# Attention on one core: value products in blocks of four steps, eight probability tiles

## The chip, the core and the metric

The kernel runs as one launch on one core of a Trainium2 chip. The metric is the device time of that launch in microseconds, the median of the runs. The engines are TensorE (PE, with its weight loads shown apart as PEld), VectorE (DVE), ScalarE (ACT), GpSimd (POOL) and SyncE (SP, which issues the DMAs); each works through its own queue in order and they meet at semaphores.

## The reference

Two batches of 2048 tokens with 256 features pass through an attention block and then a two-layer local-attention and MLP block, each inside an adaptive layer norm. The change touches only the first attention:

```python
x: (2, 2048, 256); 16 heads of 64
h = layernorm(x) * (1 + ca) + sa
q, k, v = heads(h @ Wq + bq), heads(h @ Wk + bk), heads(h @ Wv + bv)
pattern = einsum('bhid,bhjd->bhij', k, q) / 8
prob = softmax(pattern, axis=-2)          # over the keys i
out = einsum('bhis,bhid->bhsd', prob, v)
x = x + ga * (concat(out) @ Wo + bo)
# then: layernorm, and a gated block of two layers of windowed attention and gated MLP
```

## The kernel before

**Phases.** A start-up (input, first projections, the first head's maxima), then attention, then the second layer norm and the two layers. Only attention is written by the code that changes. It takes 32 heads one after the other (2 batches by 16 heads); two heads are a pair, `hh` 0 and 1, and there are 16 pairs. `PLAN` has four kinds of pair: FIRST, MIDDLE (13 of them, in hardware loops), BRIDGE (the last of batch 0, which also turns the next batch's hidden tokens into `hT`), LAST.

**A head.** The 2048 queries are taken in two halves (`cp` 0 and 1) of 1024, the 2048 keys in 16 tiles of 128 (`kt`), so a head has 32 steps (`STEPS`). For a step:

- `scores`: four matmuls of 512 columns on the whole 128x128 array (L1430 and L1431, reduced-precision fp32, the high part and the low part of the operands), into one of two pairs of PSUM banks. Step t waits for the exponentials of step t-2, which free its banks.
- ScalarE takes one exponential of 128x1024 (L848) and writes `prob[t % PRING]`. It waits for the tile to be free again: the value products of step t-PRING and the addition of that tile.
- `values`: PE multiplies the tile with `vv` (L1442), full fp32, 64 output columns, one query half on each half of the array side by side. The page counts two records for each such matmul, so a step has four records; the two halves run at the same time.
- the column sums of the softmax: VectorE adds the tiles of `SUM_DVE` (4 of 16) to `acc_d` (L1099; the first is a copy, L1101), GpSimd the others to `acc_p` (L708) and joins both (L704).

Beside this, PE prepares the next head: `max`, 64 products of one matmul each (L1402), which exist only to find the largest score of each key row; VectorE reduces each from PSUM (L1076, 128x512). At a head's end all 64 are reduced once more, turned (`turn`, L1408), negated (`max_neg`, L1086) and sent by a DMA of SP (`qlm<-nmx`) into row 64 of `qlm`; the next head's first scores wait for it. `proj_qk` projects queries and keys for the head after next (four items of four records, L1379; ScalarE and VectorE read them, L799 to L802 and L1037 to L1039), `proj_v` the values for the next pair (L1387), `out` the output projection of the pair before (8 items, L1461 and L1120), `sum` turns an accumulator into column sums (L1451, ones times `accp`), and VectorE then takes the reciprocal (L1105, 128x512) and scales `o_raw` into `oT` (L1110): `normalise`.

**The ring.** `max`, `sum`, `turn`, `turn_h`, `proj_v` and `out` share three PSUM banks (`RING = 3`) in the order of the plan. PE may write an item only when VectorE has finished the item three places before it (`ring_slot`). For `sum` that is the end of the second L1110.

**The order.** `head_order` writes one list for a head, and PE and VectorE both follow it. Before the change it has 16 groups of two steps: two score steps, with maxima ahead, between and behind (`mm S m S mm` in most groups, where S is a score step and m a maximum), and then two value steps (`VV`). VectorE's addition stands where the values stand. `sum` of half 0 stands behind group 10, and group 11 has no maxima (but in BRIDGE, where it has `mm S m S m` and a turned tile), group 12 two or three, group 15 none: there the order is turn, the four `proj_qk`, `VV`, and for `hh` 1 `proj_v`, then `sum` of half 1.

## Time and profile before

| | us |
|---|---|
| median of 3 runs | 4878.4 (4864.67 to 4885.79) |
| the profiled execution: its own time | 4883.0 |
| its span in the profile | 4881.1 |
| attention, first value product to last | 100.9 to 3148.4 |
| PE busy over the span | 4565.5 (94%) |
| DVE / ACT / POOL busy | 3426.1 / 2212.1 / 2728.9 |
| granted TensorE clock, mean | 0.971 |

The page's busy time of PE is a union of modelled spans: a 512-column matmul is drawn with 0.40 us though the next starts 0.23 us later, so a PE that looks busy can still be losing time. What it loses is read from the distance between starts in the timeline.

### The profile page before, as it was taken

To read this page: it belongs to the slowest core of one execution; us is meant where nothing else is said; L and a number is where in the kernel's file an instruction comes from. 1 tells how busy PE (TensorE), PEld (TensorE's weight loads), DVE (VectorE), ACT (ScalarE), POOL (GpSimd) and SP (SyncE) were. 2 spreads that over 40 slices of the span, in tenths; PEclk is the share of its full clock that TensorE was granted. 3 is DMA by queue.
4 is the path that set the end of the run, shared out by engine and by line. 5 is a ranking of instruction groups with operands and counts; after the bars stand their busy time and mean duration, and the time that the engine had idled before them with its cause. 6 is when DMAs were issued, how large, how long until landed. Compare 5 with 4: busy or idle time off the path is not lost.

```text
span 4881.1 us, 65202 instructions
## 1 busy us (share of the span) xinstructions
PE 4565.5 (94%) x21552; PEld 2792.1 (57%) x21552; DVE 3426.1 (70%) x4564; ACT 2212.1 (45%) x3535; POOL 2728.9 (56%) x1172
## 2 busy tenths in 40 slices
PE   7999999999999999999999999858999897999898
PEld 5555555555555555555555555426766675777576
DVE  7887878778788788787787787565555454666354
ACT  5444444444444444444444444325665343656442
POOL 3655656566556665675666565606666223666322
PEclk9999999999999999999999999979999998999898
DMA  2000000000000000000000000010000100000001
GB/s 65 1 5 5 2 6 1 6 6 1 6 5 2 5 1 6 6 1 6 5 2 6 5 2 2 1 56 1 1 1 1 36 1 18 1 1 1 1 0 35
DMA packets 56826, 37.55 MB, mean 8 GB/s; under 512 B 32572, under 2 KB 55056, under 8 KB 56464
## 3 DMA queue, kind: packets, MB, share of 16 engines
q1 hardware_dynamic: 56464, 33.02, 2.3%
q8 instruction: 191, 3.13, 0.3%
q14 instruction: 171, 1.40, 0.1%
HBM read 28.54 MB, written 4.19 MB: 7 GB/s over the span
## 4 chain that ended last, share of the span: by engine, by line
POOL 48%; issue 26%; PE 13%; DVE 7%; ACT 4%; POOLq 1%; DMA 0%; DVEq 0%; SPq 0%; ACTq 0%
POOL accp L708 36%; PE psum L1705 4%; POOL lp L730 4%; PE psum L1580 3%; POOL accp L704 3%; POOL rnorm L720 2%; POOL qk_u L725 2%; DVE ssq L1180 1%; ACT lp L894 1%; PE psum L1626 1%; ACT qk_sq L878 1%; PE psum L1718 1%; DVE qk_w L1192 1%; DVE lneg L1206 1%; PE psum L411 1%
## 5 line engine op out<-in xcount | busy, mean ns | idle before, releaser
L708 POOL TENSOR_TENSOR accp<-accp,prob 128x1024 f32<-128x1024 f32 x640 | 1618.9, 2530 | 684.3 <-ACT prob L848 651.9
L848 ACT ACTIVATE prob<-psum 128x1024 f32<-128x1024 f32 x1024 | 1042.7, 1026 | 1547.4 <-PE psum L1431 1395.8
L1076 DVE TENSOR_REDUCE mx<-psum 128x1 f32<-128x512 f32 x1984 | 1276.0, 684 | 420.3 <-PE psum L1402 354.7
L1442 PE MATMUL psum<-prob,vv 128*64 128x512 f32 x4096 | 996.0, 607 | 0.0
L1430 PE MATMUL psum<-qhh,klh 128*128 128x512 f32 x2048 | 829.4, 405 | 39.8 <-issue 20.7
L1431 PE MATMUL psum<-qlm,kh 65*128 65x512 f32 x2048 | 818.0, 399 | 0.0
L1402 PE MATMUL psum<-klh,qhh 128*128 128x512 f32 x1984 | 711.3, 419 | 14.2 <-DVE mx L1076 10.0
L1402 PEld LDWEIGHTS psum<-klh,qhh 128*128 128x128 f32 x1984 | 347.9, 190 | 413.9 <-DVE mx L1076 245.4
L1442 PEld LDWEIGHTS psum<-prob,vv 128*64 128x64 f32 x4096 | 249.5, 136 | 513.1 <-issue 370.2
L1430 PEld LDWEIGHTS psum<-qhh,klh 128*128 128x128 f32 x2048 | 392.2, 191 | 199.8 <-issue 87.2
L1431 PEld LDWEIGHTS psum<-qlm,kh 65*128 65x128 f32 x2048 | 391.7, 191 | 91.7 <-issue 7.0
L730 POOL TENSOR_TENSOR lp<-lp,lrcp 128x1024 f32<-128x1024 f32 x128 | 301.0, 2352 | 229.8 <-DVE lrcp L1212 229.8
L1099 DVE TENSOR_TENSOR accd<-accd,prob 128x1024 f32<-128x1024 f32 x192 | 398.9, 2078 | 21.5 <-ACT prob L848 20.4
L708 POOL TENSOR_TENSOR accp<-prob 128x1024 f32<-128x1024 f32 x64 | 152.9, 2389 | 378.9 <-ACT prob L848 373.8
L720 POOL TENSOR_TENSOR rnorm<-ssc,minus_half 128x16 f32<-128x16 f32 x64 | 186.0, 2906 | 291.2 <-DVE ssc L1182 291.2
L758 POOL TENSOR_TENSOR ug_l<-uf,ug_h 128x512 fp32r<-128x512 f32 x96 | 128.6, 1339 | 387.3 <-ACT ug_h L969 387.3
L894 ACT ACTIVATE lp<-psum,lneg 128x256 f32<-128x256 f32 x512 | 236.1, 481 | 98.8 <-DVE lneg L1206 98.8
L1105 DVE RECIPROCAL psum<-psum 128x512 f32<-128x512 f32 x64 | 215.1, 3360 | 27.8 <-PE psum L1451 27.1
L1379 PE MATMUL psum<-hT,wqk 128*128 128x512 f32 x512 | 226.4, 594 | 0.0
L1626 PE MATMUL psum<-identf,lp 128*128 128x128 f32 x1024 | 144.6, 286 | 57.6 <-POOL lp L730 57.6
L1180 DVE TENSOR_REDUCE ssq<-qk_sq 128x16 f32<-128x1024 f32 x64 | 78.1, 1220 | 169.7 <-ACT qk_sq L878 169.6
L704 POOL TENSOR_TENSOR accp<-accp,accd 128x1024 f32<-128x1024 f32 x64 | 151.7, 2371 | 72.4 <-DVE accd L1099 72.1
(190 smaller groups left out, 6534.1 us busy)
## 6 DMA issues: line engine op xcount, KB each, us to landing
rot_l<-const_rot SPq DMA_DIRECT2D x2, 2048.0 KB, 8.5
out<-lpT SPq DMA_DIRECT2D x32, 128.0 KB, 1.8
wqkv_l<-L_ffn_wqkv SPq DMA_DIRECT2D x4, 768.0 KB, 9.7
w_l<-L_ffn_w SPq DMA_DIRECT2D x4, 682.0 KB
wqk<-L_attn_Wq SPq DMA_DIRECT2D x32, 64.0 KB, 2.1
wqk<-L_attn_Wk SPq DMA_DIRECT2D x32, 64.0 KB, 2.0
wv_p<-L_attn_Wv SPq DMA_DIRECT2D x16, 128.0 KB, 2.2
wo_p<-L_attn_Wo SPq DMA_DIRECT2D x16, 128.0 KB, 2.0
```

The costliest lines, as they stand in the source:

```text
L704: pool.tensor_tensor(acc_p[cp][:], acc_p[cp][:], acc_d[cp][:], ALU.add).then_inc(pool_sum, 1)
L708: pool.tensor_tensor(acc_p[cp][:], first[:], prob[kt % PRING][:], ALU.add).then_inc(pool_sum, 1)
L720: pool.tensor_tensor(rnorm[:], ssc[:], minus_half[:, 0:1].broadcast_to([P, 2 * LHEADS]), ALU.pow).then_inc(rn_done, 1)
L730: pool.tensor_tensor(lp[:, hs, :], lp[:, hs, :], lrcp[:, hs].unsqueeze(2).broadcast_to([P, IH, 2 * WIN]), ALU.mult).then_inc(lp_done, 1)
L848: act.activation(prob[t % PRING][:], psum[:, S_BANK + 2 * (t % 2):S_BANK + 2 * (t % 2) + 2, :].rearrange("p a b -> p (a b)"), ACT.Exp, sca ...
L894: op = act.activation(lp[:, hh, :], psum[:, 2 * it + h // 2, (h % 2) * 2 * WIN:(h % 2 + 1) * 2 * WIN], ACT.Exp, bias=lneg[:, hh:hh + 1], s ...
L1076: dve.tensor_reduce(mx4[:, j // CHUNKS, j % CHUNKS:j % CHUNKS + 1], ps, AX_X, ALU.max).then_inc(ring_free, 1)
L1099: dve.tensor_tensor(acc_d[cp][:], acc_d[cp][:], prob[kt % PRING][:], ALU.add).then_inc(dve_sum, 1)
L1402: pe.matmul(ps, qhh[s][:, qt * P:(qt + 1) * P], klh[s][:, c * T:(c + 1) * T], start=True, stop=True).then_inc(ring_full, 1)
L1430: pe.matmul(ps, klh[s][:, keys], qhh[s][:, cols], start=True, stop=False)
L1431: mm = pe.matmul(ps, kh1[s][:, keys], qlm[s][:, cols], start=False, stop=True)
L1442: mm = pe.matmul(psum[j * DH:(j + 1) * DH, O_BANK, :], vv[:, kt, s * DH:(s + 1) * DH], prob[t % PRING][:, j * T:(j + 1) * T], start=(kt == ...
```

## The change

- `PRING` goes from 4 to 8. The four new tiles take the place in SBUF of the start-up's `x_tail` and one `squares`, which now lie in `prob` 4 to 7; so ScalarE waits for `h1_ok` before the first exponential.
- A group has four steps (`VALUES = 4`): 8 groups a head. In a full group the order is `S mmm S mm S mmm S mm`, VectorE's addition (`a`), `VVVV`, for 10 maxima (9 and two `out` in the four groups that have them, 11 in group 5 of `hh` 0, 5 to 7 in group 0, 6 or 7 in group 6, 3 or 4 in group 7).
- `sum` of half 0 stands behind group 5, after value step 23 (before: after step 21). In group 0 and in group 6 the maxima come late: `S S m S mm S mmm` in group 6 of `hh` 1 (6 maxima), `S S m S mmm S mmm` in that of `hh` 0 (7).
- The additions of VectorE have places of their own in the order (`("add", t)`), ahead of the group's value products; in the last group ahead of `proj_qk`.
- The last group has maxima, and ends `a`, two `proj_qk`, turn, two `proj_qk`, `VVVV`; the value products of the last four steps all lie behind the projections (before: two ahead of them and two behind).
- In BRIDGE the eight turned tiles go two to a group, in groups 3 to 6; the outputs stay in groups 1 to 4, two to each.

Here `a` is an addition and `V` the value products of one step. The diff:

```diff
--- before.py
+++ after.py
@@ -35,7 +35,7 @@
 KT = N // P
 CP = CHUNKS // 2
 STEPS = CP * KT
-PRING = 4
+PRING = 8
 SUM_DVE = (2, 5, 8, 12)
 SUM_POOL = tuple(k for k in range(KT) if k not in SUM_DVE)
 
@@ -172,13 +172,12 @@
         mx1 = sb("mx1", [P, KT], at=att)
         nmx = sb("nmx", [KT, P], F32R, at=att)
         wmod_sb = hT[:, :, 0:6 * D]
-        x_tail = sb("x_tail", [P, 12, D], at=att)
         st_sum = sb("st_sum", [P, KT], at=att)
         st_neg = sb("st_neg", [P, B, KT], at=att)
         st_ssq = sb("st_ssq", [P, B, KT], at=att)
         st_var = sb("st_var", [P, B, KT], at=att)
         st_rs = sb("st_rs", [P, B, KT], at=att)
-        squares = [sb("squares", [P, 2, D], at=att), o_raw[0][:].rearrange("p (t d) -> p t d", d=D)]
+        squares = [prob[7][:, 0:2 * D].rearrange("p (t d) -> p t d", d=D), o_raw[0][:].rearrange("p (t d) -> p t d", d=D)]
         copies = o_raw[1][:].rearrange("p (t d) -> p t d", d=D)
 
 
@@ -186,7 +185,7 @@
             return t[:].rearrange("p (t d) -> p t d", d=D)
 
         x_quads = [[quad(t) for t in acc_p + acc_d],
-                   [x_tail[:, 4 * q:4 * q + 4, :] for q in range(3)] + [x_last[:]]]
+                   [quad(t) for t in prob[4:7]] + [x_last[:]]]
         h_quads = [[quad(t) for t in prob], [h_next[:, 4 * q:4 * q + 4, :] for q in range(QUADS)]]
         wo_all = oT[:].rearrange("p (k n) -> p k n", n=D)
         att.close()
@@ -294,49 +293,61 @@
 
 
 
-        GROUPS = STEPS // 2
-        SUM0_GROUP = (KT + 5) // 2
-
-        def max_places(outs):
-
-
-            weight = [4] * (GROUPS - 1) + [0]
-            weight[0] = 1
-            weight[SUM0_GROUP + 1:SUM0_GROUP + 3] = [0, 2]
-            for g in outs:
-                weight[g] = 3
+        VALUES = 4
+        GROUPS = STEPS // VALUES
+        SUM0_GROUP = (KT + 5) // VALUES
+        OUT_GROUPS, OUT_EACH = 4, 2
+        TURN_EACH = 2
+
+        def max_places(outs, turns):
+
+
+            weight = [10] * GROUPS
+            weight[0], weight[SUM0_GROUP + 1], weight[GROUPS - 1] = 5, 6, 4
+            for g in (*outs, *turns):
+                weight[g] -= 2
             return [-(-RING_MAX * sum(weight[:g + 1]) // sum(weight)) for g in range(GROUPS)]
 
+        def spread(g, n, count):
+
+            ends = [0, n // 5, 3 * n // 5, n] if g in (0, SUM0_GROUP + 1) else [-(-n * (j + 1) // count) for j in range(count)]
+            return list(zip([0] + ends, ends))
+
         FIRST, MIDDLE, BRIDGE, LAST = 0, 1, 2, 3
-        TURN_GROUP = 1 + WO_ITEMS // 2
+        TURN_GROUP = 3
 
         def head_order(which, hh):
             last = which == LAST
             maxima, projects = not (last and hh), not last
-            outs = () if which == FIRST or hh else range(1, 1 + WO_ITEMS // 2)
-            turns = range(TURN_GROUP, TURN_GROUP + TWINS) if which == BRIDGE and hh == 0 else ()
-            placed = max_places([*outs, *turns])
+            outs = () if which == FIRST or hh else range(1, 1 + OUT_GROUPS)
+            turns = range(TURN_GROUP, TURN_GROUP + TWINS // TURN_EACH) if which == BRIDGE and hh == 0 else ()
+            placed = max_places(outs, turns)
             order = [("scores", 0), ("scores", 1)]
             for g in range(GROUPS):
                 upto = placed[g] if maxima else 0
                 done = (placed[g - 1] if g else 0) if maxima else 0
                 tiles = [("max", j) for j in range(done, upto)]
                 if g in outs:
-                    tiles += [("out", 2 * (g - 1)), ("out", 2 * (g - 1) + 1)]
+                    tiles += [("out", OUT_EACH * (g - 1) + j) for j in range(OUT_EACH)]
                 if g in turns:
-                    tiles.append(("turn_h", g - TURN_GROUP))
-
-                n = len(tiles)
-                cut0 = (n + 1) // 3
-                cut1 = cut0 + n // 3
+                    tiles += [("turn_h", TURN_EACH * (g - TURN_GROUP) + j) for j in range(TURN_EACH)]
+
+                adds = [("add", t) for t in range(VALUES * g, VALUES * (g + 1)) if t % KT in SUM_DVE]
                 if g + 1 < GROUPS:
-                    order += tiles[:cut0] + [("scores", 2 * g + 2)] + tiles[cut0:cut1] + [("scores", 2 * g + 3)] + tiles[cut1:]
+                    for j, (lo, hi) in enumerate(spread(g, len(tiles), VALUES)):
+                        order += [("scores", VALUES * (g + 1) - 2 + j)] + tiles[lo:hi]
+                    order += adds
                 else:
+                    for j, (lo, hi) in enumerate(spread(g, len(tiles), 2)):
+                        order += [("scores", STEPS - 2 + j)] + tiles[lo:hi]
+                    order += adds
+                    if projects:
+                        order += [("proj_qk", i) for i in range(2)]
                     if maxima:
                         order.append(("turn", 0))
                     if projects:
-                        order += [("proj_qk", i) for i in range(QK_ITEMS)]
-                order += [("values", 2 * g), ("values", 2 * g + 1)]
+                        order += [("proj_qk", i) for i in range(2, QK_ITEMS)]
+                order += [("values", VALUES * g + j) for j in range(VALUES)]
                 if g == SUM0_GROUP:
                     order.append(("sum", 0))
             if projects and hh == 1:
@@ -835,6 +846,8 @@
                 act.wait_ge(oT_ready, G * CP + cp + 1)
                 act.activation(o_raw[cp][:], psum[:, O_BANK, :], ACT.Copy).then_inc(o_free, 1)
 
+            act.wait_ge(h1_ok, QUADS - 1)
+
             def exps(G):
                 for t in range(STEPS):
                     act.wait_ge(s_full, G * STEPS + t + 1)
@@ -1132,10 +1145,9 @@
                             max_neg(G + 1, rb, r, TURN_PLACES[hh])
                         elif kind == "turn_h":
                             next_hidden(rb, r, j, places(kind, j, hh))
-                        elif kind == "values":
+                        elif kind == "add":
                             cp, kt = divmod(j, KT)
-                            if kt in SUM_DVE:
-                                add_sum(G, cp, SUM_DVE.index(kt))
+                            add_sum(G, cp, SUM_DVE.index(kt))
                         elif kind == "sum":
                             normalise(G, rb, r, hh, j)
                         elif kind == "proj_qk":
```

## Rows read from the trace of the kernel before

**Rows 1.** The page: busy time of each engine, share of the span, instructions.

```profile
PE 4565.5 (94%) x21552; PEld 2792.1 (57%) x21552; DVE 3426.1 (70%) x4564; ACT 2212.1 (45%) x3535; POOL 2728.9 (56%) x1172
```

**Rows 2.** Windows, 500 us of attention: PE, PEld, DVE, ACT, POOL; clock.

```profile
1000.00:1500.00 500.00, 490.47 (x2014) 269.07 (x2013) 400.96 (x508) 217.71 (x242) 308.71 (x124) 1.00 0.02 4
```

**Rows 3.** Waits of PE from 100 to 3075 us: us, times, longest.

```profile
PE psum L1430 <- issue: 20.7, 16, 1.7
PE psum L1430 <- DVE klh L1039: 14.0, 15, 0.9
PE psum L1402 <- DVE mx L1076: 10.0, 12, 1.1
```

**Rows 4.** Timeline of PE, one full group of two steps: start, us, instruction.

```profile
1700.10 1.94 PE L1442 MATMUL psum<-prob,vv 128*64 128x512 f32 x8
1701.96 0.72 PE L1402 MATMUL psum<-klh,qhh 128*128 128x512 f32 x2
1702.53 0.40 PE L1430 MATMUL psum<-qhh,klh 128*128 128x512 f32 x1
...
1704.63 0.63 PE L1402 MATMUL psum<-klh,qhh 128*128 128x512 f32 x2
1705.19 1.94 PE L1442 MATMUL psum<-prob,vv 128*64 128x512 f32 x8
```

**Rows 5.** Timeline of PE: values behind an output; a sum behind values.

```profile
1657.33 1.88 PE L1461 MATMUL psum<-oT,wo_p 128*128 128x512 f32 x4
1659.14 0.65 PE L1442 MATMUL psum<-prob,vv 128*64 128x512 f32 x2
...
1710.52 1.94 PE L1442 MATMUL psum<-prob,vv 128*64 128x512 f32 x8
1712.29 0.60 PE L1451 MATMUL psum<-accp,ones 128*64 128x512 f32 x2
```

**Rows 6.** Timeline around the BRIDGE pair's sum of half 0.

```profile
1513.71 1.03 PE L1451 MATMUL psum<-accp,ones 128*64 128x512 f32 x4
...
1514.67 0.73 PE L1402 MATMUL psum<-klh,qhh 128*128 128x512 f32 x2
1514.79 3.37 DVE L1105 RECIPROCAL psum<-psum 128x512 f32<-128x512 f32 x1
1515.24 0.40 PE L1430 MATMUL psum<-qhh,klh 128*128 128x512 f32 x1
...
1516.52 1.02 ACT L848 ACTIVATE prob<-psum 128x1024 f32<-128x1024 f32 x1 [3.96 <-PE psum L1431]
1518.19 1.38 DVE L1110 TENSOR_TENSOR oT<-o_raw,psum 64x512 f32<-64x512 f32 x2
1519.62 0.80 PE L1402 MATMUL psum<-klh,qhh 128*128 128x512 f32 x1 [3.30 <-DVE oT L1110]
```

**Rows 7.** Timeline: VectorE's additions and maxima, and PE behind them.

```profile
1104.99 2.09 DVE L1099 TENSOR_TENSOR accd<-accd,prob 128x1024 f32<-128x1024 f32 x1
...
1107.00 3.73 DVE L1076 TENSOR_REDUCE mx<-psum 128x1 f32<-128x512 f32 x6
...
1107.28 0.95 PE L1402 MATMUL psum<-klh,qhh 128*128 128x512 f32 x2
...
1274.56 3.44 DVE L1099 TENSOR_TENSOR accd<-accd,prob 128x1024 f32<-128x1024 f32 x1
```

**Rows 8.** Windows behind the BRIDGE wait and at a junction of heads.

```profile
1519.00:1526.00 7.00, 6.38 (x18) 3.47 (x18) 4.14 (x7) 1.02 (x1) 2.34 (x1) 0.51 0.00 0
...
1157.00:1164.00 7.00, 5.96 (x25) 3.11 (x23) 6.59 (x6) 4.55 (x5) 2.88 (x2) 1.00 0.00 0
```

**Rows 9.** Timeline: the projections' start and VectorE's end of the second item.

```profile
1146.68 3.60 PE L1379 MATMUL psum<-hT,wqk 128*128 128x512 f32 x8
...
1153.86 0.76 DVE L1039 SCALAR_TENSOR_TENSOR klh<-psum,bqk,klh 64x512 fp32r<-64x512 f32 x1
```

**Rows 10.** DMA issues, 1000 to 2000 us: count, KB each, median us to landing.

```profile
qlm<-nmx SPq DMA_DIRECT2D x10, 8.0 KB, 1.8
```

## The prediction

> **What bounds the kernel now.** I began with the page's busy times: PE is busy 94% of the span, the others at most 70% [rows 1]. Windows say where: in 500 us of attention PE shows 490 us busy at a clock of 1.00, VectorE 401, GpSimd 309, ScalarE 218 [rows 2]. Attention is some 3,050 of the 4,881 us, nothing else is edited in a way that counts, and there the end is set by PE: 32 heads of about 95 us. The chain of waits names GpSimd at 48%, but it runs through short waits of an engine that is only 62% busy in that window; I don't use it. So the question is what each microsecond of PE goes to.
>
> The waits view gives PE three frequent releasers in attention, 45 us in all [rows 3], and one wait of 3.3 us in BRIDGE, which is taken up below. That is small. The larger loss is inside the "busy" time, and shows in the distance between starts [rows 4]. From one value block to the next are 5.09 us. In it: 8 score and 5 maximum matmuls at 0.233 us (1702.53 to 1704.63 is 2.10 for nine), 3.03 us; 8 value records, which are 4 slots of 0.43 (the side-by-side halves share a slot), 1.72. That leaves 0.34. It lies in four places: the last maximum before the values starts at 1704.86 (0.63 less the 0.40 of one) and the values at 1705.19, 0.33 instead of 0.23; the first value slot takes 0.05 more (1.94 - 0.60 is 1.34 for three slots); the last value slot starts at 1701.44, the maximum at 1701.96, 0.52 instead of 0.43; and the next matmul comes after 0.32 instead of 0.23. It is the change of array width, not of number type: fp32 output tiles at full width to values is also 0.52 (1657.33 + 1.88 - 0.59 to 1659.14), while values to sums, both 64 columns wide, is 1.77 for four slots with no extra at the end [rows 5].
>
> **The change, part by part.** Sums are against the profiled execution: 4883.0, span 4881.1.
>
> *A. Half as many value blocks.* 16 round trips a head become 8: 8 x 32 x 0.34 = 87 us less. The Trainium skill (TensorEngine Tiling (Array Packing), Key Properties) says that a change of tiling mode drains the engine; the trace agrees in kind. The phase drawing in "TensorE: Matmul & The Clock Gate" gives a drain of some 128 cycles; two drains at 2.4 GHz would be 0.11 us a round trip and 27 us in all, called an estimate. The rows measure 0.34, so the sum stays with 87.
>
> *B. The ring behind the sum of half 0.* The BRIDGE pair shows what maxima close behind a sum cost [rows 6]. The sum's last slot starts at 1514.14 (call it u). The reciprocal starts at u+0.65, takes 3.37, the scaling ends at 1519.57, and the third maximum, which needs the sum's bank, starts at 1519.62 = u+5.48, after 3.30 us of idle PE. In the old MIDDLE order nothing of this is seen, since a score pair and a value block lie between.
> Now for the new group 6, `S S m S mmm S mmm` or `S S m S mm S mmm`. From u: S at 0.52 to 1.56, S to 2.49, m. The third S needs the exponential of the first: a score step starts at 1515.24, its exponential at 1516.52 and takes 1.02 [rows 6]; with the 0.1 of the width change it ends at u+2.94, S starts at 3.0 instead of 2.72. S ends at 4.03, the second m at 4.27, and the third waits to 5.50: 1.2 us. The last S and m follow. VectorE then works through three waiting maxima at 0.60 each (3.73 for six [rows 7]), and PE gets each bank 0.73 after its reduction starts, which adds 0.3 (`hh` 1) or 0.5 (`hh` 0, whose fourth maximum comes at once). The first matmul after each stop takes another 0.1. Together 2.0 us for `hh` 1 and 2.4 for `hh` 0, where the old order lost 0.2 and 0. 15 x 1.8 + 16 x 2.4 = 65 us more; BRIDGE's old stop and the slow clock behind it, 6 us, come back: 59 us. Bounds: 0 if neither wait lasts, 3.3 a head as in BRIDGE, 102 us.
>
> *C. The ring inside full groups.* PE makes three maxima in 0.7 us, then one S of 0.93; VectorE reduces one in 0.60. In `S mmm S mmm S mmm S out out` the first m starts at 1.04, VectorE at 1.47; the sixth maximum wants to start at 3.13 and gets its bank at 3.40, the ninth is 0.07 late; with 0.1 after each, 0.5 us. 60 such groups: 31 us. 15 groups of 11: 8 us. Groups of 10: the eighth is 0.06 late, 0.16 us, 80 groups, 13 us. Against it stand the old stops. An addition pushed VectorE past the start of the next group: it ends at 1107.08, the maxima queue to 1110.73, and two maxima of PE lie 0.55 apart instead of 0.23 [rows 7]. Beside GpSimd an addition takes up to 3.44 us, and that gave the longest stops of 1.1 [rows 3, 7]. Now an addition has 3.58 us of values and over a microsecond of scores behind it before the next maximum arrives, so these go: 10 + 12 x 0.17 from the waits, and some 13 us of short ones (12 of 0.33, 22 smaller), 25 us. C is 27 us more; bounds 0 (VectorE absorbs it) and 52.
> VectorE's load per full group: 10 x 0.60 + 2.1 = 8.1 us of 9.9. It does not become the bound.
>
> *D. The junction of heads.* Behind `hh` 0 the second S waited for the last projection's reader, L1039, 15 times, 14 us of idle [rows 3]; with the 0.17 hidden in each, the 0.1 behind it and 0.3 for an exponential, 1.5 us a head. Four value steps instead of two now lie behind the projections, 1.7 us more, so the wait for L1039 goes. But no maximum stands between the first scores any more, and the third S waits for exponential 0: by the times of B 0.6, and 0.2 to 0.3 later. Net 0.65 x 16 = 10 less. Behind `hh` 1, at the loop's end, 16 waits by "issue" of 1.3 on the mean stay [rows 3], and one more exponential is waited for, 0.3 a pair, 5 us. D: 5 us less.
> The turn moves behind two projections. `max_neg` now stands behind VectorE's second projection item, which ended 7.94 us after the first projection started (1154.62 to 1146.68 [rows 9]); with its own 0.3 that is 8.2. The store lands 1.8 us after its issue [rows 10], so with 0.3 between the two it is there at 10.3, and the scores come at 11.6 (four items of 1.72, turn, four value steps, sum). It costs nothing, with 1.3 us of cover; behind it on SP stand only the next pair's loads, which have a whole head of time.
>
> *E. Eight tiles.* With more tiles ScalarE waits less for VectorE and GpSimd. Worth 0 by itself: ScalarE is 44% busy [rows 2], and scores stay two steps ahead of it, bound by their PSUM banks. GpSimd's work does not change, and it is 62% busy. ScalarE's wait for `h1_ok` and the shared start-up tiles: 0; those were read long before. *F.* The last head has no maxima: in `SSSS VVVV` the third S wants to start at 1.97 and waits for an exponential to 2.5, 0.6 a group with the 0.1 behind it, less A's 0.34: 2 us more.
>
> Sum: -87 + 59 + 27 - 5 + 2 = -4 us, about 4879 for a profiled execution like this one. That execution stood 4.6 us above the median of the runs, so about 4874. The large gain is spent on waits that the new order makes.
>
> **Rivals.**
> 1. *The gain stays.* The waits of B are shorter, since the order of maxima shifts load or the exponentials come sooner, and C is absorbed. For: VectorE has 18% spare in each full group, and value blocks of 3.6 us let both it and GpSimd catch up. Against: in BRIDGE the wait for the bank lasted 3.3 us whatever else was free. Without B: 4815. Without C too: 4788. Half of B and C: 4831. I take 4820.
> 2. *Slower: the clock falls.* Behind BRIDGE's wait the granted clock is 0.51 for 7 us, the lower level of 1.2 GHz; behind an `hh` 0 junction with one stop of 1.3 it stays 1.00 [rows 8]. Group 6 now stops three or four times for 2.0 to 2.4 us in all, in 31 heads. A low stretch of 6.8 us costs 3.4. It decides from about 8 low stretches on (27 us); 13 give 4874 + 44 = 4918. The Trainium skill (TensorE: Matmul & The Clock Gate, Why this matters for your kernels) warns that gaps between bursts of matmuls bring the slow clock back; BRIDGE agrees.
> 3. *A late store or sum.* The turn is later, half 1's sum behind GpSimd's join of a later addition. With 1.3 us of cover gone and 1.5 more lost in 16 to 31 heads: 24 to 46 us, 4905.
>
> **How the numbers follow.** A measurement of this kernel tells 0.5%, 24 us, from no change. Forecast (gain and waits even, 4855 to 4895): 0.43, point 4874. Rival 1: 0.34. Rival 2: 0.14. Rival 3: 0.09. Faster: rival 1's share with the forecast's lower edge, 0.36; slower 0.21; same 0.43. The range takes in rival 1's middle and rival 2's: 4800 to 4918.
>
> **What would show it.** Value blocks of 16 records, 3.58 us long, and 8 a head: right for A. Third maximum behind the sum of half 0 at u+5.5, waits of PE on `DVE oT L1110` near 1 us x 31: right for B; if that row is absent, B is wrong and rival 1 holds. Waits on `DVE mx` of some 60 to 150 times, short: C. The L1039 wait gone: D. More stretches of 0.5 clock than before: rival 2. A DMA `qlm<-nmx` or `POOL accp L708` among PE's releasers: rival 3. I am wrong if a full group of 10 maxima is not near 9.9 to 10.0 us.

## The result: slower, by 1.2%

The changed kernel takes 4939.3 us (median of 4 runs, 4934.7 to 4944.0), the kernel before 4882.1 in the same session. The ratio is 1.0122, 95% interval 1.0097 to 1.0147: 57 us slower, where the forecast was no change that can be measured, 4874, and a range that ended at 4918. The profiled executions differ by 52.8 us in span.

First the page of the changed kernel: the span, each engine's busy time, and the costliest matmul groups (with the idle time of PE ahead of them and what ended it). It answers to [rows 1].

```profile
span 4933.9 us, 65082 instructions
...
PE 4563.0 (92%) x21552; PEld 2809.2 (57%) x21552; DVE 3416.9 (69%) x4564; ACT 2212.5 (45%) x3535; POOL 2691.2 (55%) x1172
...
L1454 PE MATMUL psum<-prob,vv 128*64 128x512 f32 x4096 | 942.1, 602 | 0.0
L1442 PE MATMUL psum<-qhh,klh 128*128 128x512 f32 x2048 | 857.1, 419 | 55.4 <-issue 20.0
...
L1414 PE MATMUL psum<-klh,qhh 128*128 128x512 f32 x1984 | 671.9, 419 | 51.4 <-DVE oT L1123 34.5
```

Instruction counts are equal on every engine, and the busy times differ by 1.4% at most, so no engine has more work than before. A new entry stands behind the maxima: 34.5 us of idle PE that ended with `DVE oT L1123`, the end of the normalisation (L1110 before). The waits of PE in attention, 100 to 3220 us (total us, times, longest), answer to [rows 3]:

```profile
PE psum L1414 <- DVE oT L1123: 34.5, 31, 1.2
PE psum L1442 <- issue: 20.0, 16, 1.7
PE psum L1442 <- ACT prob L861: 13.4, 43, 0.4
PE psum L1442 <- DVE klh L1052: 8.8, 15, 0.8
PE psum L1463 <- POOL accp L719: 7.9, 2, 5.4
PE psum L1442 <- DMA qlm<-nmx: 7.8, 13, 0.7
PE psum L1414 <- DVE mx L1089: 6.4, 17, 0.4
```

Three rows are new in kind: the 31 waits for the bank of the sum (one a head but the last), 13 for the DMA into `qlm`, and 43 for an exponential (13.4 us; before, one of 0.2), which the forecast had counted inside B and D. One is still there that was to go: the 15 waits for L1052, the reader of the last projection (L1039 before). The old waits on `DVE mx` of up to 1.1 us are down to 0.4.

**Where the time went.** As in [rows 4], the distance from one value block to the next is read against its parts: 0.233 us a score or maximum matmul, 0.43 a slot of values or a full-fp32 record, 0.11 a small transpose or value projection, 0.35 for the change of array width and back. What is left is called excess. It can be worked out for every group from the starts in the timeline, and includes waits, the 0.1 us behind a wait and slow-clock stretches. A junction is the stretch from a head's last value products to the next head's first. Over attention, in us (the first row counts blocks):

| | before | after | difference | forecast |
|---|---|---|---|---|
| value blocks (a sum beside one counted with it) | 526 blocks | 271 blocks | -255 x 0.35 = -88 | -87 (A) |
| excess, groups with the sum of half 0 and what follows | 9 | 87 | +78 | +59 (B) |
| excess, full groups, and the last group's scores | 23 | 61 | +38 | +27 (C) |
| excess, junctions of heads | 60 | 82 | +22 | -5 (D) |
| last pair, and widths around the projections | 3 | 8 | +5 | +2 (F) |
| attention | | | +55 | -4 |

The profile's own sum agrees: from its first value product to its last, attention takes 3102.1 us where it took 3048.0, 54 more. It begins 3.2 us later, since two more score steps stand ahead of the first value product, and what stands behind it is 4.6 us shorter. Part A is there in full. A full group of ten maxima, PE alone, whose length was the test named in the forecast:

```profile
1012.27 3.65 PE L1454 MATMUL psum<-prob,vv 128*64 128x512 f32 x16
1015.86 0.50 PE L1442 MATMUL psum<-qhh,klh 128*128 128x512 f32 x1
...
1016.90 0.86 PE L1414 MATMUL psum<-klh,qhh 128*128 128x512 f32 x3
...
1019.96 1.01 PE L1414 MATMUL psum<-klh,qhh 128*128 128x512 f32 x3
...
1022.29 0.65 PE L1454 MATMUL psum<-prob,vv 128*64 128x512 f32 x2
```

It is 10.02 us for four steps, against two groups of 5.09 (10.18) before. Three maxima normally span 0.86; the second three span 1.01, since the eighth waits for its bank: 0.05, and 0.1 behind it. Such stops hardly show as idle time, since a matmul is drawn with 0.40 us and the next starts after 0.23: the list of waits has only 17 waits on `DVE mx`, where the forecast named 60 to 150 as the sign of C. They stand in the distances between starts.

Now group 6 of a head `hh` 1. It answers to [rows 6]; PE, VectorE and the exponential:

```profile
1233.68 1.03 PE L1463 MATMUL psum<-accp,ones 128*64 128x512 f32 x4
1234.64 0.50 PE L1442 MATMUL psum<-qhh,klh 128*128 128x512 f32 x1
1234.76 3.37 DVE L1118 RECIPROCAL psum<-psum 128x512 f32<-128x512 f32 x1 [2.26 <-PE psum L1463]
...
1236.04 1.96 ACT L861 ACTIVATE prob<-psum 128x1024 f32<-128x1024 f32 x2 [5.04 <-PE psum L1443]
...
1236.63 0.39 PE L1414 MATMUL psum<-klh,qhh 128*128 128x512 f32 x1
1237.12 0.50 PE L1442 MATMUL psum<-qhh,klh 128*128 128x512 f32 x1
...
1238.25 1.39 DVE L1123 TENSOR_TENSOR oT<-o_raw,psum 64x512 f32<-64x512 f32 x2
...
1239.69 0.50 PE L1414 MATMUL psum<-klh,qhh 128*128 128x512 f32 x1 [1.12 <-DVE oT L1123]
...
1240.97 1.32 PE L1414 MATMUL psum<-klh,qhh 128*128 128x512 f32 x3
```

With u = 1234.11 (the sum's last slot), the third maximum starts at u+5.58; before it the third score step (1237.12) waited 0.26 for an exponential, and the last three maxima span 1.32 instead of 0.86.

### The profile page after: what moved, and what is told of

Same layout as the page of the kernel before. It is cut to its first block, busy times and chain, and to the rows that moved or that the text cites. A ratio compares the mean times of both kernels' runs of the same rounds, so it can differ in the third digit from the quotient of the medians.

```text
span 4933.9 us, 65082 instructions
## 1 busy us (share of the span) xinstructions
PE 4563.0 (92%) x21552; PEld 2809.2 (57%) x21552; DVE 3416.9 (69%) x4564; ACT 2212.5 (45%) x3535; POOL 2691.2 (55%) x1172
## 4 chain that ended last, share of the span: by engine, by line
POOL 46%; issue 28%; PE 13%; DVE 7%; ACT 4%; POOLq 1%; DMA 0%; DVEq 0%; SPq 0%; ACTq 0%
POOL accp L719 35%; PE psum L1717 4%; POOL lp L741 4%; PE psum L1592 3%; POOL accp L715 3%; POOL rnorm L731 2%; POOL qk_u L736 2%; DVE ssq L1192 1%; ACT lp L907 1%; PE psum L1638 1%; ACT qk_sq L891 1%; PE psum L1730 1%; DVE qk_w L1204 1%; DVE lneg L1218 1%; PE psum L422 1%
## 5 line engine op out<-in xcount | busy, mean ns | idle before, releaser
L719 POOL TENSOR_TENSOR accp<-accp,prob 128x1024 f32<-128x1024 f32 x640 | 1577.0, 2464 | 676.9 <-ACT prob L861 630.9
L1089 DVE TENSOR_REDUCE mx<-psum 128x1 f32<-128x512 f32 x1984 | 1225.3, 682 | 485.0 <-PE psum L1414 470.1
L1454 PE MATMUL psum<-prob,vv 128*64 128x512 f32 x4096 | 942.1, 602 | 0.0
L1442 PE MATMUL psum<-qhh,klh 128*128 128x512 f32 x2048 | 857.1, 419 | 55.4 <-issue 20.0
L1414 PE MATMUL psum<-klh,qhh 128*128 128x512 f32 x1984 | 671.9, 419 | 51.4 <-DVE oT L1123 34.5
L1454 PEld LDWEIGHTS psum<-prob,vv 128*64 128x64 f32 x4096 | 273.1, 138 | 568.5 <-issue 519.6
L1414 PEld LDWEIGHTS psum<-klh,qhh 128*128 128x128 f32 x1984 | 380.8, 192 | 262.6 <-DVE mx L1089 144.6
L1112 DVE TENSOR_TENSOR accd<-accd,prob 128x1024 f32<-128x1024 f32 x192 | 352.5, 1836 | 17.5 <-ACT prob L861 16.3
```

What stands on the lines that cost most here:

```text
L719: pool.tensor_tensor(acc_p[cp][:], first[:], prob[kt % PRING][:], ALU.add).then_inc(pool_sum, 1)
L1089: dve.tensor_reduce(mx4[:, j // CHUNKS, j % CHUNKS:j % CHUNKS + 1], ps, AX_X, ALU.max).then_inc(ring_free, 1)
L1112: dve.tensor_tensor(acc_d[cp][:], acc_d[cp][:], prob[kt % PRING][:], ALU.add).then_inc(dve_sum, 1)
L1414: pe.matmul(ps, qhh[s][:, qt * P:(qt + 1) * P], klh[s][:, c * T:(c + 1) * T], start=True, stop=True).then_inc(ring_full, 1)
L1442: pe.matmul(ps, klh[s][:, keys], qhh[s][:, cols], start=True, stop=False)
L1454: mm = pe.matmul(psum[j * DH:(j + 1) * DH, O_BANK, :], vv[:, kt, s * DH:(s + 1) * DH], prob[t % PRING][:, j * T:(j + 1) * T], start=(kt == ...
```

## The experiments

Ratios are to the kernel before, measured beside each run; the kernel before has a median of 4881, 4872 and 4884 us in the three sessions, so ratios are compared, not times. The first four experiments are of the first session; the early addition alone and the last two experiments are of the third. Excess and low-clock stretches are read from one profiled execution of each kernel.

**The sum of half 0 ahead of the value products.**

```diff
                         order += [("scores", VALUES * (g + 1) - 2 + j)] + tiles[lo:hi]
+                    if g == SUM0_GROUP:
+                        order.append(("sum", 0))
                     order += adds
...
                 order += [("values", VALUES * g + j) for j in range(VALUES)]
-                if g == SUM0_GROUP:
-                    order.append(("sum", 0))
```

> The changed kernel with the sum of half 0 (and its normalisation on VectorE) moved ahead of group 5's value products and ahead of that group's addition; nothing else. Theory W (the loss is VectorE's 5.5 us behind this sum, which hold the ring's third bank, with the slow-clock stretches that follow): the four value steps now cover the reciprocal. The 31 waits of PE on DVE oT (34.5 us of idle) fall below 0.4 each, group 6 comes down from 12.0 and 13.5 us to near 10 and 10.5, and the run is 55 to 80 us faster than the changed kernel: 4860 to 4885. Rival C (the loss is the clock, which falls because the scores and exponentials come in bursts between long value blocks): no less than 10 low stretches stay in attention and the run stays above 4915. Rival P (long value blocks themselves starve PE at the head junctions and in full groups): the run stays above 4915 with the oT waits gone.

Measured: 4873.2, ratio 0.9981 (0.9971 to 0.9992), 1.4% below the changed kernel and just below the kernel before. The waits on `DVE oT` are gone from the list; group 6 with its sum and values is down from a mean of 12.0 us (`hh` 1) and 13.4 (`hh` 0) to 10.2 and 10.8, its excess from 2.2 and 3.4 to 0.4 and 0.8. The timeline shows why: the reciprocal and the scaling lie under the value block.

```profile
1208.50 1.08 PE L1463 MATMUL psum<-accp,ones 128*64 128x512 f32 x4
1209.40 3.61 PE L1454 MATMUL psum<-prob,vv 128*64 128x512 f32 x16
...
1209.62 3.37 DVE L1118 RECIPROCAL psum<-psum 128x512 f32<-128x512 f32 x1
1212.94 0.50 PE L1442 MATMUL psum<-qhh,klh 128*128 128x512 f32 x1
1213.11 1.39 DVE L1123 TENSOR_TENSOR oT<-o_raw,psum 64x512 f32<-64x512 f32 x2
...
1214.81 1.22 DVE L1112 TENSOR_TENSOR accd<-accd,prob 128x1024 f32<-128x1024 f32 x1 [0.31 <-DVE oT L1123]
```

The low-clock stretches in attention fall from 18 (72 us) to 11 (61 us), not below 10; the kernel before has 7 (44 us). The bursts and the long value blocks of rivals C and P are untouched by this edit, and the time went all the same: both fall as main causes.

**The turn ahead of all projections.**

```diff
-                    if projects:
-                        order += [("proj_qk", i) for i in range(2)]
                     if maxima:
                         order.append(("turn", 0))
                     if projects:
-                        order += [("proj_qk", i) for i in range(2, QK_ITEMS)]
+                        order += [("proj_qk", i) for i in range(QK_ITEMS)]
```

> The changed kernel with the turn of the maxima ahead of all four projections, as in the kernel before; nothing else. Theory W: the 13 waits of PE on the DMA into qlm (7.8 us of idle) go, but the second score step still waits for VectorE's reader of the last projection, so 5 to 15 us faster than the changed kernel: 4924 to 4934; it may lose 1.5 us a head at the turn itself, since VectorE must first reduce the last maxima, which would make it 4940 to 4975. Rival (the late store is the main loss at the junctions): over 20 us faster.

Measured: 4971.9, ratio 1.0187 (1.0170 to 1.0204), 0.6% above the changed kernel; the second branch of the expectation. PE now waits for VectorE to reduce the last maxima:

```profile
PE psum L1418 <- DVE mx L1092: 39.4, 31, 1.6
PE psum L1412 <- DVE oT L1121: 34.6, 31, 1.2
```

What I had not expected is in what is missing: with the turn late, both the DMA wait and the 15 waits for the projection's reader are gone, and the junction behind `hh` 0 has an excess of 1.0 instead of 2.3. The projections start 1.4 to 2.3 us later behind the addition here, and VectorE's first copy behind `hh` 0 takes 0.43 us instead of 2.42. So the reader was late because of what VectorE did ahead of it; which part of it is taken up below.

**Eight tiles alone.** The kernel before with

```diff
-PRING = 4
+PRING = 8
...
+            act.wait_ge(h1_ok, QUADS - 1)
+
             def exps(G):
```

and the start-up's tiles laid over `prob` 4 to 7 as in the change.

> The kernel before with eight probability tiles in place of four (and the start-up's tiles laid over them), the order of the work untouched. Theory W: ScalarE's waits for a free tile go, the few PE stops of about 1.1 us that hang on them or on long additions may go too: 0 to 12 us faster than the kernel before. Rival L (the new place of the tiles in SBUF or the start-up wait costs time): 10 us or more slower than before.

Measured: 4882.2, ratio 1.0006 (0.9996 to 1.0015). The tiles, their place and the start-up wait cost and give nothing. The waits on `DVE mx` fall from 10.0 us in 12 to 4.8 in 8, which is less than the measurement can tell.

**A short reciprocal.**

```diff
-                dve.reciprocal(ps, ps).then_inc(rcp_ok, 1)
+                if cp == 0:
+                    dve.reciprocal(ps[:, 0:1], ps[:, 0:1]).then_inc(rcp_ok, 1)
+                else:
+                    dve.reciprocal(ps, ps).then_inc(rcp_ok, 1)
```

> The changed kernel with the reciprocal of half 0's sums taken of one column instead of 512, so half the heads' outputs are not normalised; it leaves out that arithmetic and about 3.3 us of VectorE a head, and keeps every place and wait. Theory W: the ring's bank comes free at about 2.2 us after the sum's last slot instead of 5.5, the oT waits vanish, only the wait for the exponential (0.4 a head) stays in group 6: 60 to 80 us faster than the changed kernel, 4860 to 4880. Rivals C and P: less than 25 us faster.

Measured: 4867.4, ratio 0.9973 (0.9963 to 0.9983), 1.5% below the changed kernel. Two edits of different kinds, one that hides the 3.4 us and one that leaves them out, give nearly the same 1.4 and 1.5%, and the same excess in group 6 (0.40 and 0.75). That makes B shown.

**The last addition ahead of the maxima**, on top of the early sum, and later on the changed kernel alone.

```diff
                     for j, (lo, hi) in enumerate(spread(g, len(tiles), 2)):
-                        order += [("scores", STEPS - 2 + j)] + tiles[lo:hi]
-                    order += adds
+                        order += [("scores", STEPS - 2 + j)] + (adds if j == 0 else []) + tiles[lo:hi]
```

> The kernel with the early sum (e1_sum_early, 4873), and in the last group VectorE's addition ahead of the maxima, behind the first of the two score steps. Theory J (the junction of heads lost what the sum did not show, because the addition in front of the projections makes VectorE late: the join on GpSimd then starts with VectorE's first copy of a projection, which took 2.4 us instead of 0.4 to 1.1): the copy comes down to about 0.5, VectorE ends the projections 1 to 2 us sooner, so the 15 waits on the last projection's reader (8.7 us of idle) and the 13 waits on the store of the maxima (7.8 us) go or halve, and the run is 10 to 25 us faster than e1_sum_early: 4848 to 4863. Rival S (the store alone is late, since the turn stands behind two projections, and the copy's length is not what counts): no more than 5 us faster.

> The changed kernel with only the last group's addition moved ahead of that group's maxima; the sum of half 0 stays where the change put it. Theory J: VectorE's first copy of a projection no longer runs beside GpSimd's join, the waits on the last projection's reader and on the store of the maxima go (16.6 us of idle, some 20 with what hides behind), 10 to 25 us faster than the changed kernel, so 1.0 to 1.4% above... that is, between 4914 and 4929 where the changed kernel has 4939. Rival S: no more than 5 us faster.

Measured: with the early sum 4853.4, ratio 0.9966 (0.9955 to 0.9978), 0.15% or 7 us below the early sum alone, where theory J had 10 to 25; alone 4929.0, ratio 1.0094 (1.0079 to 1.0110), 0.28% or 14 us below the changed kernel, as expected. Both pairs of intervals overlap, so the times alone show little. The traces are clearer. With the early sum, the junction behind `hh` 0 goes from an excess of 2.3 to 1.0, and of the 15 waits for the reader one is left and of the 13 for the DMA none. Alone, 14 short waits for the reader stay (3.8 us, 0.5 at most), the DMA's go. With the early sum, some 5 us of the gain are given back at once in the last group of `hh` 0, whose maxima now queue behind the addition (0.4 a head). Here is the place in the changed kernel, GpSimd's join and VectorE's copy, then the two waits of PE:

```profile
1160.81 1.56 DVE L1112 TENSOR_TENSOR accd<-accd,prob 128x1024 f32<-128x1024 f32 x1
...
1162.45 2.35 POOL L715 TENSOR_TENSOR accp<-accp,accd 128x1024 f32<-128x1024 f32 x1 [1.16 <-DVE accd L1112]
...
1162.66 2.42 DVE L1050 CAST kh<-klh 64x512 fp32r<-64x512 f32 x1 [0.29 <-ACT klh L811]
...
1169.46 0.56 SPq L575 DMA_DIRECT2D qlm<-nmx  x1
...
1171.55 0.47 PE L1442 MATMUL psum<-qhh,klh 128*128 128x512 f32 x1 [0.63 <-DMA qlm<-nmx]
...
1173.31 0.47 PE L1442 MATMUL psum<-qhh,klh 128*128 128x512 f32 x1 [0.58 <-DVE klh L1052]
```

**Maxima dealt 2, 3, 2, 3.**

```diff
-            ends = [0, n // 5, 3 * n // 5, n] if g in (0, SUM0_GROUP + 1) else [-(-n * (j + 1) // count) for j in range(count)]
+            ends = [0, n // 5, 3 * n // 5, n] if g in (0, SUM0_GROUP + 1) else [n * (j + 1) // count for j in range(count)]
```

> e1_sum_early with the maxima of a full group dealt as 2, 3, 2, 3 in place of 3, 2, 3, 2 (2, 3, 3, 3 in place of 3, 3, 3, 2 where there are eleven tiles). Theory W (the stops in full groups are the ring of three against VectorE's 0.60 us a maximum): groups of ten lose their 0.18 us, 80 times, and those with eleven tiles lose 0.2 to 0.5 of their 0.55, 70 times: 20 to 40 us faster than e1_sum_early, 4833 to 4853. Rival (these stops come from something that the places of the maxima don't set): within 5 us of e1_sum_early.

Measured: 4866.1, ratio 0.9990 (0.9981 to 1.0000): not faster than the early sum (0.9981). My expectation failed. The output groups went from 0.56 to 0.40, but the plain groups of ten stay at 0.18 and only the one with the sum got worse (0.20 to 0.25 on the mean of all), those of eleven went from 0.64 to 0.86, and the early sum now waits for a bank 30 times (6.8 us): the stop moved to the last triple of the group. I had left the 0.43 us from a maximum to VectorE's start out of one step of the count.

**All of these, and a maximum between the second and third score step.**

```diff
+                    early = 1 if g == 0 and tiles else 0
+                    order += tiles[:early]
...
-                        order += [("scores", VALUES * (g + 1) - 2 + j)] + tiles[lo:hi]
+                        order += [("scores", VALUES * (g + 1) - 2 + j)] + tiles[max(lo, early):max(hi, early)]
```

> The early sum, the early addition and the evenly dealt maxima together, and the first maximum of a head between its second and third score step, as in the kernel before. If the pieces add up: 35 to 70 us faster than e1_sum_early, 4803 to 4838, and so 0.9 to 1.6% below the kernel before. If the junctions and the full groups share one cause, less than the sum of the two.

Measured: 4854.8, ratio 0.9963 (0.9949 to 0.9977), the same as the early sum and addition (0.9966), and 9 us below the early sum where 35 to 70 were expected if the pieces add up. The dealing adds nothing, as in the run before. The junction behind `hh` 0 is 1.04 with and without the maximum in between; it fills a wait and then shows elsewhere.

**Two value blocks again.** The early sum with

```diff
+                        if j == VALUES - 1:
+                            order += [("values", VALUES * g), ("values", VALUES * g + 1)]
                         order += [("scores", VALUES * (g + 1) - 2 + j)] + tiles[lo:hi]
...
-                order += [("values", VALUES * g + j) for j in range(VALUES)]
+                order += [("values", VALUES * g + j) for j in range(2 if g + 1 < GROUPS else 0, VALUES)]
```

> e1_sum_early with the value block of each group but the last cut in two, one half ahead of the group's last score step; the same work in nearly the same order, seven more changes of array width and back in each head. Theory W: each costs 0.34 us of PE, 7 x 32 x 0.34 = 76 us slower than e1_sum_early: 4935 to 4965 with what waits move. Rival (the width change is hidden where PE has other waits, or the cost is in the number type, which changes as often in both): less than 30 us slower.

Measured: 5035.7, ratio 1.0330 (1.0314 to 1.0346), 3.5% above the early sum. Attention is 167 us longer. That is 70 us beyond the expected range. 224 more blocks at 0.35 are 78; the 80 half groups in which PE waits for nothing (`VV S mm`, 3.47 us) are just the sum of their parts with that 0.35. The other 88 are excess, for which the expectation had left too little: the sum is followed by half the cover (3.3 us of excess in `hh` 0), PE waits for VectorE's maxima 47 times (45.7 us), and VectorE gets no long pause. The size of A stands, and in this order, with eight or nine maxima between two half blocks, the long value block is worth as much again by the cover that it gives to VectorE. It is not so in every order: the kernel before has blocks of two steps too, and little excess in its full groups, with its maxima dealt for them. Rival P has it the wrong way round.

**Tiles dealt by VectorE's pace.** The early sum and addition with

```diff
             ends = [0, n // 5, 3 * n // 5, n] if g in (0, SUM0_GROUP + 1) else [-(-n * (j + 1) // count) for j in range(count)]
+            if count == VALUES and n in (10, 11) and g not in (0, SUM0_GROUP + 1):
+                ends = [3, 5, n - 3, n]
...
                     tiles += [("out", OUT_EACH * (g - 1) + j) for j in range(OUT_EACH)]
+                    if g not in turns:
+                        tiles = tiles[:2] + tiles[-2:-1] + tiles[2:6] + tiles[-1:] + tiles[6:-2]
```

> e5_add_first (early sum, early addition) with the tiles of a full group dealt by VectorE's pace: 3, 2, 2, 3 maxima behind the four score steps (3, 2, 3, 3 for eleven), and the two outputs of an output group among the maxima, as third and eighth tile, in place of both at the end. By the times of the traces (0.60 us a maximum on VectorE, a bank free 0.73 us after its reduction starts) no maximum of these groups then comes before its bank. Theory W: the 0.55 us in 56 output groups, the 0.6 in 14 groups of eleven and most of the 0.2 in 80 groups of ten go, 30 to 50 us faster than e5_add_first. Rival (each group has a stop wherever the maxima stand, as in e6_even_maxima, since VectorE's queue and not the places sets it): less than 10 us faster.

Measured: 4819.5, ratio 0.9872 (0.9857 to 0.9887): 1.3% below the kernel before and 0.94% below the step ahead of it, 46 us, as expected. An output group of it, PE alone:

```profile
1239.86 3.65 PE L1457 MATMUL psum<-prob,vv 128*64 128x512 f32 x16
...
1244.48 0.63 PE L1417 MATMUL psum<-klh,qhh 128*128 128x512 f32 x2
1244.95 1.02 PE L1476 MATMUL psum<-oT,wo_p 128*128 128x512 f32 x2
...
1248.61 1.03 PE L1476 MATMUL psum<-oT,wo_p 128*128 128x512 f32 x2
...
1250.40 0.86 PE L1417 MATMUL psum<-klh,qhh 128*128 128x512 f32 x3
1251.19 0.65 PE L1457 MATMUL psum<-prob,vv 128*64 128x512 f32 x2
```

11.33 us, the sum of its parts, where the changed kernel has 11.88. Groups of ten are at 0.04 in most places (0.13 on the mean), groups of eleven still at 0.64. The profiled attention is 2982 us, some 120 of them excess: 35 less than the step before. The rest of the 46 is no more than the intervals of the two ratios (6 and 7 us) leave open.

**Group 6 as a full group.**

```diff
-            weight[0], weight[SUM0_GROUP + 1], weight[GROUPS - 1] = 5, 6, 4
+            weight[0], weight[GROUPS - 1] = 5, 4
```

and the late start of the maxima kept for group 0 only.

> e9_dealt with group 6 as a full group (with the sum's reciprocal covered there is no reason to keep maxima away), so the other groups have nine or ten maxima instead of ten or eleven. Theory W: group 6 loses its 0.4 (hh 1) and 0.76 (hh 0), the others have more air: 10 to 20 us faster than e9_dealt. Rival: the third maximum of group 6 meets the sum's bank again, 10 us or more slower.

Measured: 4842.7, ratio 0.9919 (0.9905 to 0.9932), 0.5% or 23 us slower than the step before. The rival holds in effect, with another releaser:

```profile
PE psum L1417 <- DVE mx L1092: 24.8, 31, 0.8
```

The bank of the sum is free, but VectorE has 3.4 + 1.4 us of normalisation and then an addition in its queue before the first maximum, and the ring of three is full behind it: 1.65 us of excess where the thin group had 0.40 and 0.75. The thin group behind the sum was a good part of the change.

## Why the prediction was wrong

**What bounds the kernel, and A: right.** The loss of PE inside its "busy" time was real, 0.35 a round trip, and 255 fewer of them are 88 us (forecast 87). The trace agrees with the Trainium skill's rule that a change of tiling mode drains the engine (TensorEngine Tiling (Array Packing), Key Properties); the prediction's estimate of 27 us is a third of what was measured. The split blocks confirm the size.

**The failed step is D.** The forecast said that the wait for L1039 "goes", that the moved turn costs nothing "with 1.3 us of cover", and summed D to 5 us less. It came to 22 us more, 27 off: 12 more behind `hh` 0, where I had 10 less, and 11 more behind `hh` 1, where I had 5.

Behind `hh` 0, I carried VectorE's time for the projections (7.94 us to the end of the second item) over from the old order. There GpSimd's join is nearly over when VectorE's first copy starts:

```profile
1147.94 2.35 POOL L704 TENSOR_TENSOR accp<-accp,accd 128x1024 f32<-128x1024 f32 x1 [1.17 <-DVE accd L1099]
...
1150.01 0.56 DVE L1037 CAST kh<-klh 64x512 fp32r<-64x512 f32 x1 [1.95 <-ACT klh L800]
```

In the new order the addition runs until 1162.37, 3.0 us into the projections, GpSimd's join starts with its end, and the copy runs beside the join for 2.42 us. The second item then ended at 1169.13, 9.8 us after the first projection started (1159.33), the store was issued at 1169.46, and both waits came. So rival 3 was partly true and stood with 0.09.

It is the copy's length that makes the reader late, and not the addition by itself. In all of these runs the copy starts 3.33 us after the first projection, because it waits for ScalarE's `klh`, and the addition is over by then; it ends 0.28 us behind the end of the join that it started inside; and the second item ends 4.0 us behind the copy. Medians behind `hh` 0:

| kernel | copy, us | second item ends, us after the first projection | waits of PE for the reader | for the DMA |
|---|---|---|---|---|
| before | 0.56 | 7.94 | 15, 14.0 us (old order) | none |
| early sum and addition | 0.99 | 8.35 | 1, 0.6 us | none |
| early addition alone | 1.42 | 8.79 | 14, 3.8 us | none |
| changed | 2.41 | 9.79 | 15, 8.8 us | 13, 7.8 us |

The Trainium skill (GPSIMD Engine Reference, Specifications) says that GpSimd's SBUF interfaces are shared with VectorE, with contention for VectorE instructions that run in a 2-port mode or have two SBUF inputs. The trace agrees that the two collide; the copy has one input, and in which mode it ran no run here shows.

Behind `hh` 1 there is no such lateness. In a pair without the loop end's waits the excess went from 0.82 to 1.75: two waits for an exponential, 0.34 and 0.38 us, and what follows a wait, where I had priced one more at 0.3. No experiment takes these away.

**B, mis-sized: 59 forecast, 78 measured.** The mechanism was right to a tenth: third maximum at u+5.5 (5.58), wait for the exponential 0.27 (0.26), 31 waits near 1.1. The shortest group is at 2.10 (`hh` 1) and 2.60 (`hh` 0) where I had 2.0 and 2.4. The mean of `hh` 0 is 3.4, because behind its longer stop the clock falls in 12 of 15 heads. A window there (busy us of PE, PEld, DVE, ACT, POOL, then the granted clock):

```profile
1149.00:1152.00 3.00, 2.77 (x8) 2.00 (x8) 2.35 (x5) 0.65 (x1) 1.69 (x1) 0.66 0.00 0
```

A granted clock of 0.66 over 3 us is a part at 1.2 and a part at 2.4 GHz, behind 1.11 us of idle PE and then 0.41. At half speed the low stretches cost 17 us in the groups with this sum, where they cost 2 before: most of the 19. Rival 2 was thus true in part: 18 low stretches of 72 us together in attention against 7 of 44, which at half speed is 14 us of the 55.

**C, mis-sized by 11: 27 forecast, 38 measured.** Output groups 0.55 (0.5), groups of ten 0.18 (0.16), groups of eleven 0.54 (0.5). The last group of `hh` 0 has 0.45 on the mean, 6 us in all, which I had not counted. It is the clock again: PE waits for nothing there, the heads without a low stretch have no excess, and in the others the stretch began in group 6 and runs over. With the sum early, or its reciprocal short, it is 0.00. The 23 us of old stops did go.

**E right**, by the run with eight tiles alone. **F** small, as forecast.

The sum of errors: 27 in D, 19 in B, 11 in C, 3 beside F, less 1 in A: 59, from -4 to +55. In D behind `hh` 0 the place was followed on PE, with VectorE taken as on time. Most of the 19 in B and 6 of the 11 in C are the slow clock behind the stops, which stood under rival 2 and not in the sum.

## What to carry to other kernels

When a busy TensorE alternates array widths, count the round trips (0.35 us each here) and pay them less often; but a longer block is also cover, so put the other engine's longest serial work (here reciprocal and scaling, 4.8 us) at its start and not behind its end. When work is reordered, follow the second engine's queue through each place, with what GpSimd does beside it: durations taken over from the old order are the ones that fail, and here a copy that started under a GpSimd addition ended only behind it. A ring of three is emptied at VectorE's pace (0.60 us), so deal the tiles by that pace, with the items that cost PE most (outputs, 0.86 us) among those that it could issue fastest.

## What was not expected of the hardware

- A VectorE copy of 64x512 (fp32 to reduced fp32) takes 0.42 us alone. Started inside a GpSimd addition of 128x1024 that takes 2.35, it ends 0.28 us behind the end of that addition, however long that is: 0.56, 0.99, 1.42 or 2.42 us. Behind `hh` 1 of the changed kernel the copy starts 0.01 us ahead; then it takes 0.42, and the GpSimd addition is the longer one:

```profile
1251.82 0.42 DVE L1050 CAST kh<-klh 64x512 fp32r<-64x512 f32 x1
1251.83 2.63 POOL L715 TENSOR_TENSOR accp<-accp,accd 128x1024 f32<-128x1024 f32 x1 [1.16 <-DVE accd L1112]
```

- In group 6 of the changed kernel the half-clock stretch came behind two stops of 1.1 and 0.4 us within 1 us of each other, in 12 of 15 heads `hh` 0; in three the same stops left the clock at 1.00. Behind the stop of 1.0 to 1.1 of `hh` 1, with no more than 0.1 after it, it stayed at 1.00 in all 16.
- The first matmul after any stop of PE, even of 0.05 us, is followed by the next one after 0.33 instead of 0.23 us: a short wait costs 0.1 more than it lasts.
- Behind `hh` 1 PE stands still once or twice for some 1.3 us by "issue" in 11 of 15 pairs, 16 waits and 20 to 22 us in every version; no edit of the order touched it, and its cause stays open.
